# Block two of a two-block metaformer: first scores ahead of the projection, convolution inside the causal attention, combination in nine pieces

## The reference

```python
x = x + _L0_conv_ref(_ln_c(x), ...)      # block one: 7 x 7 neighbourhood attention, 12 heads
t = _to_tokens(x)
t = t + _L0_ffn_ref(_ln_t(t), ...)       # 32 experts, 6 per token, capacity 48, and a shared one
x = _from_tokens(t, x)
x = x + _L1_conv_ref(_ln_c(x), ...)      # block two: full attention within an image, 12 heads
t = _to_tokens(x)
t = t + _L1_ffn_ref(_ln_t(t), ...)       # a causal attention, then 16 experts, 2 per token
```

## Time and profile before

| | |
|---|---|
| median of three runs | 1199.09 us (1198.32 to 1204.48) |
| the profiled execution | 1204.88 us, of which the span 1202.9 us |
| PE busy | 84% of the span |
| DVE, ACT, POOL busy | 60%, 41%, 27% |
| granted clock of PE, mean | 0.945 of full speed |
| chain that ended last | PE 43%, DVE 22%, issue 17%, ACT 6%, POOL 5%, DMA 5% |

### The profile page before, as it was taken

One profiled execution on the slowest core, in us unless ns is written; L12 is line 12 of the kernel. 1 busy time (PEld: TensorE's weight loads), 2 busy tenths in 40 slices (PEclk: granted clock), 3 DMA queues, 4 the chain that ended last, 5 costly groups with the idle time before them and its releaser, 6 DMA issues.

```text
span 1202.9 us, 25715 instructions
## 1 busy us (share of the span) xinstructions
PE 1010.0 (84%) x9398; PEld 789.2 (66%) x9398; DVE 724.5 (60%) x2245; ACT 492.9 (41%) x1223; POOL 319.6 (27%) x514
## 2 busy tenths in 40 slices
PE   4799999999998799788778888787877768989991
PEld 3576776767776545486566657575755547979891
DVE  6586686776774334446576777777776674423334
ACT  1452543643634122115365554555555554212220
POOL 0000000000000470625444554636301120423331
PEclk8999999999998899989899999999997978999996
DMA  9151350540531999600000000000000019698945
GB/s 345 30 150 40 109 148 4 145 140 8 148 110 39 266 364 420 226 1 1 1 2 1 19 1 19 2 19 1 19 1 19 5 34 370 253 396 298 313 148 174
DMA packets 68852, 144.04 MB, mean 120 GB/s; under 512 B 4864, under 2 KB 55184, under 8 KB 66592
## 3 DMA queue, kind: packets, MB, share of 16 engines
q1 hardware_dynamic: 64208, 132.23, 32.5%
q0 software_dynamic: 4560, 10.69, 2.7%
HBM read 96.69 MB, written 46.20 MB: 119 GB/s over the span
## 4 chain that ended last, share of the span: by engine, by line
PE 43%; DVE 22%; issue 17%; ACT 6%; POOL 5%; DMA 5%; POOLq 0%; DVEq 0%; ACTq 0%; SPq 0%
PE bank L1890 8%; DVE neg_max L741 5%; PE bank L641 4%; DMA R<-in_ffn_gu 4%; PE bank L592 4%; PE bank L663 3%; PE bank L705 3%; PE bank L2027 2%; PE bank L1918 2%; POOL sorted_x L1099 2%; PE bank L838 2%; DVE R L714 2%; PE bank L845 2%; ACT R L770 2%; PE bank L671 2%
## 5 line engine op out<-in xcount | busy, mean ns | idle before, releaser
L770 ACT ACTIVATE R<-bank,neg_max 128x128 f32<-128x128 f32 (+2 forms) x576 | 189.1, 404 | 131.4 <-DVE neg_max L741 131.2
L1087 POOL TENSOR_SCALAR R<-cf,ids_rel 128x128 bf16<-128x128 f32 x256 | 168.4, 678 | 39.5 <-PE bank L2007 39.0
L641 PE MATMUL bank<-cf,R 128*128 128x128 f32 x864 | 139.4, 286 | 34.3 <-ACT R L779 20.3
L741 DVE TENSOR_REDUCE neg_max<-bank 128x2 f32<-128x352 f32 (+2 forms) x216 | 129.8, 608 | 29.4 <-PE bank L624 24.0
L641 PEld LDWEIGHTS bank<-cf,R 128*128 128x128 f32 x864 | 98.3, 146 | 56.3 <-ACT R L770 43.2
L1039 POOL TENSOR_TENSOR rstd<-mean_var,cf 128x2 f32<-128x2 f32 x24 | 4.7, 195 | 459.9 <-DVE mean_var L901 459.9
L793 ACT ACTIVATE R<-bank 128x1024 bf16<-128x1024 bf16 x72 | 70.5, 1020 | 74.2 <-PE bank L592 73.9
L1890 PE MATMUL bank<-R 64*116 64x256 f32 (+1 forms) x512 | 97.7, 399 | 0.0
L592 PE MATMUL bank<-cb,R 128*128 128x128 bf16 x1008 | 70.6, 233 | 21.6 <-DVE R L569 21.6
L592 PEld LDWEIGHTS bank<-cb,R 128*128 128x128 bf16 x1008 | 65.1, 105 | 28.9 <-DVE R L569 18.1
L1890 PEld LDWEIGHTS bank<-R 64*116 64x116 f32 (+1 forms) x512 | 65.2, 180 | 26.4 <-issue 16.7
(11 more groups left out here) (258 smaller groups left out, 1908.3 us busy)
## 6 DMA issues: line engine op xcount, KB each, us to landing
R<-in_ffn_w SPq DMA_DIRECT2D x48, 864.0 KB, 7.3
sorted_x<-cmp SPq DMA_DIRECT2D x8, 4128.0 KB, 16.6
R<-in_ffn_gu SPq DMA_DIRECT2D x16, 1392.0 KB, 21.6
R<-in_ffn_dn SPq DMA_DIRECT2D x16, 768.0 KB, 18.4
xs_words<-sorted_x SPq DMA_DIRECT2D x47, 129.0 KB, 5.2
R<-token_y SPq DMA_DIRECT2D x8, 384.0 KB, 6.0
rows<-R SPq DMA_DIRECT2D x8, 224.0 KB, 2.3
out_x<-x_all SPq DMA_DIRECT2D x16, 96.0 KB, 2.5
```

The costliest lines, as they stand in the source:

```text
L641: ins = nc.tensor.transpose(PT[u % 2][:, at + g * P:at + (g + 1) * P], probs[:, u % 3, g * kw + c0:g * kw + c0 + P], ident)
L741: nc.vector.tensor_reduce(neg_max[:, u % 4, 0:g], score_bank(a, u)[:, 0:g * kw].rearrange("p (g k) -> p g k", g=g), AX, ALU.max, negate=Tr ...
L770: ins = nc.scalar.activation(probs[:, u % 3, g * kw:(g + 1) * kw], score_bank(a, u)[:, g * kw:(g + 1) * kw], ACT.Exp, bias=neg_max[:, u % ...
L1087: ins = nc.gpsimd.tensor_scalar(comb_s[i % 2][:, t, j, :], cst("iota_tok"), ids_rel[:, j:j + 1], None, ALU.is_equal)
```

## The change

Block two's order is rewritten on four engines; the arithmetic and the number of its matmuls stay the same.

- The first scores of the next attention (group 0 of CAUSAL, groups 0 and 1 of WINDOW) are issued behind the output's transposes and ahead of `project`; `scores` is lifted out of `attention_pe` for it, with the number already `begun`. CAUSAL's three score banks change places.
- The head transposes are split: one group (8 matmuls) ahead of the last denominators, the rest behind them, one more group behind the projection.
- The combination runs in pieces of 5, 4, 4, 4, 4, 4, 4 and 3 units at groups 2 to 5 instead of three pieces at groups 1 to 3. The wait on `c_slots` moves from the start of `c_window` to the first of these pieces.
- The convolution moves from ahead of the causal attention into its groups 1 to 3, and uses one bank in turn, so its second and third part wait until DVE has read the part before. `w_head` moves with it.
- On DVE `weights` and `sorted_rows` move from the end of `c_causal` into the next `c_window`, behind its group 1; `causal_sums`, `m_rows`, `combine`, `w_norm`, and the reads of the convolution move as well.
- On POOL `c_root` of an image comes ahead of the scatter of the image before it, which it stood behind. On ACT the squares for that root move a group later.

```diff
-            return ((M0, S0, S1) if a is CAUSAL else (S0, S1, M0))[u % 3]
+            return ((S0, M0, S1) if a is CAUSAL else (S0, S1, M0))[u % 3]
...
-        def attention_pe(pe, a, i, extra={}):
+        def scores(pe, a, i, u):
+            t, heads, k0, kw, _, mask = a.groups[u]
+            if u >= 3:
+                await_(pe, a, "exp", i, u - 2)
+
+            if u < 2 or heads[0] % 4 == 0:
+                n = max(heads[0] // 4, u % 2 if u < 2 else 0) + 1
+                await_(pe, a, "qkTa", i, n)
+                await_(pe, a, "qkTd", i, min(n, per_image(a, "qkTd")))
...
             for u in range(a.n + 3):
-                if u < a.n:
-                    scores(u)
+                if begun <= u < a.n:
+                    scores(pe, a, i, u)
...
-            return enumerate((M0, M1) if a is WINDOW and i == 1 else (S0, S1))
+            return enumerate((S0, S1) if a is NEIGH or i == 0 else (M0, M1) if i == 1 else (O1, O1))
...
+                if i >= 2:
+                    c_scatter(i - 2)
...
-                if i >= 1:
-                    c_scatter(i - 1)
+            c_scatter(B - 2)
...
+                    before[1] = lambda: squares("h", i - 1)
+                    before[2] = lambda: c_raw(i)
...
-                    between[0].append(lambda: m_rows(i - 1))
+                    between[0] += qk_copies_dve(dve, WINDOW, i + 1)[2:]
+                    between[0].append(lambda: causal_sums(i - 1))
+                if i >= 2:
+                    between[1].append(lambda: weights(i - 2))
+                    between[1].append(lambda: sorted_rows(i - 2))
+                if i >= 1:
+                    between[2].append(lambda: m_rows(i - 1))
                 if i + 2 < B:
-                    between[3].append(lambda: combine(i + 2))
-                    between[5].append(lambda: w_norm(i + 2))
...
+                    between[6 if i else 3].append(lambda: combine(i + 2))
+                    between[8 if i else 5].append(lambda: w_norm(i + 2))
...
-                at = (1, 2, 4, 5, 6, 7, 8, 8) if i else (5, 6, 6, 6, 7, 7, 8, 8)
+                at = (2, 3, 4, 5, 6, 7, 8, 8) if i else (5, 6, 6, 6, 7, 7, 8, 8)
...
+                    between[0].append(window_sums)
+                    if i + 2 < B:
+                        between[1].append(lambda: conv_qk_dve(dve, WINDOW, brow, i + 2, (0,)))
+                        between[2].append(lambda: conv_qk_dve(dve, WINDOW, brow, i + 2, (1,)))
+                        between[3].append(lambda: conv_v_dve(dve, WINDOW, brow, i + 2))
...
-                if 1 <= i < B - 1:
-                    weights(m)
-                    sorted_rows(m)
...
-                if i >= 2:
-                    pe.wait_ge(s("c_slots"), i - 1)
...
+                def first_unit():
+                    if i >= 2:
+                        pe.wait_ge(s("c_slots"), i - 1)
+                    c_comb(i + 2, 0, 5)
...
-                    for k in range(1, 4):
-                        extra[k] = lambda k=k: piece(k)
-                if i + 2 < B:
-                    extra[(7, "transposed")] = lambda: w_head(i + 2)
+                    extra[1] = lambda: causal_qkv(i)
+                    if i + 2 < B:
+                        extra[2] = first_unit
+                        at = 5
+                        for key, units in (((2, "transposed"), 4), (3, 4), ((3, "transposed"), 4), (4, 4), ((4, "transposed"), 4),
+                                           (5, 4), ((5, "transposed"), 3)):
+                            extra[key] = lambda at=at, units=units: c_comb(i + 2, at, at + units)
+                            at += units
+                        assert at == 2 * NPAIR
                 if i >= 1:
                     extra[(8, "transposed")] = lambda: m_head(i - 1)
-
-                def free(n):
-                    if n == 0 and i + 2 < B:
-                        pe.wait_ge(s("w_xTc"), i + 3)
-                if i >= 0:
-                    extra["weighted"] = lambda: transpose_qk(pe, CAUSAL, i, free, n1=3)
-                attention_pe(pe, WINDOW, i + 1, extra)
+                extra["weighted"] = lambda: transpose_qk(pe, CAUSAL, i, n1=1)
+                extra["turned"] = lambda: transpose_qk(pe, CAUSAL, i, n0=1, n1=3)
+
+                def begin():
+                    scores(pe, CAUSAL, i, 0)
+                    transpose_qk(pe, CAUSAL, i, n0=3)
+                extra["normalised"] = begin
+                attention_pe(pe, WINDOW, i + 1, extra, 2 if i else 0)
                 project(pe, WINDOW, wproj, i + 1)
 
             def c_causal(i):
                 if i < 0:
                     transpose_qk(pe, WINDOW, 1, n0=4)
                     return
-                transpose_qk(pe, CAUSAL, i, n0=3)
+                if i + 1 == B:
+                    transpose_qk(pe, CAUSAL, i, n0=3)
+                extra = {}
+
+                def conv_0():
+                    pe.wait_ge(s("w_xTc"), i + 3)
+                    conv_qk_pe(pe, WINDOW, headT, wqkv, i + 2, (0,))
+
+                def conv_1():
+                    await_(pe, WINDOW, "read", i + 2, 1)
+                    conv_qk_pe(pe, WINDOW, headT, wqkv, i + 2, (1,))
+
+                def conv_2():
+                    await_(pe, WINDOW, "read", i + 2, 2)
+                    conv_v_pe(pe, WINDOW, headT, wqkv, i + 2)
                 if i + 2 < B:
-                    pe.wait_ge(s("w_xTc"), i + 3)
-                    await_(pe, CAUSAL, "qkTa", i, 2)
-                    conv_qk_pe(pe, WINDOW, headT, wqkv, i + 2)
-                    await_(pe, CAUSAL, "qkTa", i, 3)
-                    conv_v_pe(pe, WINDOW, headT, wqkv, i + 2)
-                extra = {}
+                    extra[0] = lambda: w_head(i + 2, O1)
+                    extra[1] = conv_0
+                    extra[2] = conv_1
+                    extra[3] = conv_2
                 if i + 1 == B:
                     extra[0] = lambda: ranks(i - 1)
                 elif i >= 1:
-                    extra[1] = lambda: logits(i - 1)
+                    extra[(1, "transposed")] = lambda: logits(i - 1)
                     extra[(10, "transposed")] = lambda: ranks(i - 1)
                 if i + 1 < B:
                     extra[(9, "transposed")] = lambda: c_head(i + 1)
+                def begin():
+                    scores(pe, WINDOW, i + 2, 0)
+                    transpose_qk(pe, WINDOW, i + 2, n0=4, n1=5)
+                    scores(pe, WINDOW, i + 2, 1)
...
-                    extra["weighted"] = lambda: transpose_qk(pe, WINDOW, i + 2, n1=4)
-                attention_pe(pe, CAUSAL, i, extra)
+                    extra["weighted"] = lambda: transpose_qk(pe, WINDOW, i + 2, n1=1)
+                    extra["turned"] = lambda: transpose_qk(pe, WINDOW, i + 2, n0=1, n1=4)
+                    extra["normalised"] = begin
+                attention_pe(pe, CAUSAL, i, extra, 1 if i + 1 < B else 0)
                 project(pe, CAUSAL, wof, i)
                 if i + 2 < B:
-                    transpose_qk(pe, WINDOW, i + 2, n0=4)
+                    transpose_qk(pe, WINDOW, i + 2, n0=5)
```

More of the change, by code:

```diff
@@ L594, in transpose_qk, with attention_pe @@
                 ins.then_inc(psem("qkT"), 1)
-        def attention_pe(pe, a, i, extra={}):
+        def scores(pe, a, i, u):
[6 more added lines that the diff above has]
+                await_(pe, a, "qkTd", i, min(n, per_image(a, "qkTd")))
+            if a is WINDOW and u == 2:
+                if i == 0:
+                    await_(pe, WINDOW, "read", 1, 2)
+                else:
+                    pe.wait_ge(s("c_u"), nth_square("h", i - 2) if i > 1 else nth_square("u", 0))
+            bank = score_bank(a, u)
+            if mask:
+                nc.tensor.matmul(bank[:, 0:len(heads) * kw], cstb("identb"), cstb(*mask, len(heads) * kw),
+                                 start=True, stop=False)
+            for g, h in enumerate(heads):
+                ins = nc.tensor.matmul(bank[:, g * kw:(g + 1) * kw], q_ap(h, t), k_ap(a, h, k0, kw),
+                                       start=not mask, stop=not mask or g == len(heads) - 1)
+            ins.then_inc(psem("scores"), 1)
+        def attention_pe(pe, a, i, extra={}, begun=0):
             def fill(key):
@@ L1255, in c_causal @@
                 before = {}
+                if i + 2 < B:
+                    before[0] = lambda: w_head(i + 2)
                 if i + 1 < B:
@@ L1628, in c_window @@
                     normed(0)
-                if i >= 1:
+                if i + 1 == B:
                     causal_sums(i - 1)
-                if i + 1 == B:
+                    weights(i - 2)
+                    sorted_rows(i - 2)
                     m_rows(i - 1)
```

60 lines of the change are left out of this document (18 added, 42 removed).

## The result

The changed kernel took 1187.74 us (median of four runs, 1184.68 to 1189.91) beside 1200.7 us for the kernel before: ratio 0.9888, with a 95% interval of 0.9857 to 0.9919. The profiled execution took 1188.06 us with a span of 1186.1. So the change is faster by 1.1%. That is inside the stated range (1186 to 1208), but at rival A's 1187, and outside the 1192 to 1204 that the forecast of 1198 had for itself.

What follows compares the result with a forecast made beforehand. PE was busiest, but DVE's order set the pace at several joints. Five periods at +0.9, -4.4 for image 6 and -1 for image 7 gave -0.9 us: 1198 against the median; own range 1192 to 1204, overall 1186 to 1208.

Steps and rivals of the forecast that it cites:

- rival A: PE's full clock holds through the causal head transposes up to the window's projection; -12.3 us, 1187, chance 0.34.
- steady periods: Images 1 to 5, each 57.83 us in six stretches: +0.9 a period at the lower clock, -1.0 at the full clock.
- Legs 1, 2, 5: Head transposes to causal projection, -0.42; on to first combination matmul, +1.18; window's projection to causal score group 4, -0.2.
- Leg 3: First combination matmul to causal head transposes: 18.79 to 17.4, -1.4, with PE idle about 0.7 and 2.5.
- Leg 4: Causal head transposes to window's projection, 3.67 before: lower clock after thin PE work gives 5.30, +1.63; full clock 3.39.
- Legs 5 and 6: Window's projection to score group 4, -0.2, and on to the next head transposes, DVE-bound, +0.1.
- Rival B: Lower clock also catches head transposes and projection after the causal attention's tail, 1.63 in six periods; 1208, chance 0.24.
- Image 6: No combination here; DVE's 3.08 wait for POOL's root goes, total recovery 5.3; with the period's +0.9, -4.4.
- The slower clock behind the wait: At image 6, an estimated 2.2 us recovered beyond DVE's 3.08 wait for the root.
- Image 7: DVE's 2.96 wait for the root goes, 2.03 of sorting comes in: -1, bounds -2 and +1.
- Image 0: The first image's period, taken at nothing within the -1 for the last image.

Runs made afterwards that it cites:

- sorting back: The changed kernel with weights and sorted_rows returned to the end of c_causal on DVE; 1180.7 us, ratio 0.9832 to the kernel before.
- repeated transposes: The changed kernel with PE repeating m_head's four transposes four more times ahead of the causal head transposes; 1188.67 us, ratio 0.9893 to the kernel before.
- second trace: The changed kernel run once more, unaltered, beside other runs on one chip; 1191.67 us, ratio 0.9906 to the kernel before.
- the convolution later: The changed kernel with the convolution's third part at group 4 instead of 3; 1189.27 us, ratio 0.9907 to the kernel before.
- POOL's order alone: The kernel before with only POOL's order changed, an image's root ahead of the previous image's scatter; 1197.17 us, ratio 0.9958.
- POOL's order of before: The changed kernel with POOL's old order, the root behind the previous image's scatter; 1216.05 us, ratio 1.0115 to the kernel before.

## Why the prediction was right, and where it was not

The direction was right, and so was the range, but the range in part by luck: it reached 1187.74 through rival A, whose condition did not come. The gain came from places that I had put at little, not from the steady periods. In us, for images 1 to 5, 6, 7 and 0, the forecast was 4.5 - 4.4 - 1 + 0 = -0.9. The change's first trace has 1.4 - 5.2 - 3.0 - 3.4 = -10.3 against the kernel before, its second one 3.9 - 6.1 - 2.1 - 3.6 = -8.0.

- **Legs 1, 2, 5** came out within 0.2 us, and leg 2's wait is shown: with the sorting back it goes (6.49 to 5.09). But I counted it in five periods, and at image 1 no rows wait to be sorted: leg 2 is 5.08 there. **Leg 3** was 0.3 longer than forecast, with the two idle gaps as named (0.56 and 1.96 against 0.7 and 2.5).
- **Leg 4** has the forecast's mechanism, shown by the repeated transposes, but its price was too high. I took the 5.30 of image 0, a leg with waits of 0.36 and 0.68 in it, in which the low clock also covered the projection. The new order has no such wait, the low stretch mostly covers the transposes alone, and the leg is 4.54. In the second trace it is 4.54 to 5.52, the last where the low stretch covers the whole leg. In the first trace leg 4 got some 4.4 us longer over five periods, not 8.2 (5 x 1.63). So the five steady periods cost 1.4 us in the first trace and 3.9 in the second, instead of 4.5.
- **Legs 5 and 6** came out as forecast, but "DVE bounds it" is too simple. At image 5, where the clock in the tail stays at 1.00, PE's wait of 0.81 does cost time (the run with the convolution later).
- **Rival A** named nearly the measured time, but the clock did not hold. **Rival B** did not come: leg 1 takes 3.7 to 3.8 in every period of the change's two traces, though the low stretch of the tail moved about.
- **The rule of the Trainium skill** ("TensorE: Matmul & The Clock Gate", section "Why this matters for your kernels"), that single gaps must be short, would have let the clock hold here. From 699.80 the clock is 0.50, behind gaps of 0.56 and 1.96; the measurement decides against the rule in this place.
- **Image 6**: -5.2, and -6.1 in the second trace, against the -4.4 forecast. POOL's swap alone gives 2.3, less than the 3.08 that I took for the least, since a wait of 0.64 is left. The lower clock that I put into its leg 4 did not come (3.33 in both traces). The slower clock behind the wait, which I put at 2.2, did get shorter. The stretches at 0.50, in the kernel before, with POOL's order alone, in the change, and in the change again:

```profile
918.00:931.50 13.50, 9.28 (x69) 5.52 (x70) 10.00 (x28) 7.56 (x24) 0.00 (x0) 0.50 0.01 2
...
916.30:926.50 10.20, 8.48 (x67) 5.12 (x68) 6.46 (x17) 5.75 (x18) 1.15 (x1) 0.50 0.09 28
...
917.70:924.40 6.70, 5.79 (x48) 3.30 (x48) 5.11 (x14) 4.30 (x14) 0.59 (x1) 0.50 0.06 22
...
919.50:922.90 3.40, 3.07 (x27) 1.98 (x28) 2.90 (x6) 2.42 (x9) 0.07 (x1) 0.50 0.11 41
```

The period gets shorter in the same order: 49.51, 47.22, 44.29, 43.39. PE was busy for 9.28 us in the first of these stretches, and for 5.79 and 3.07 in the last two. At the full clock the differences, 3.5 and 6.2, would take at least half as long, so at most 1.7 us of the 5.2 and 3.1 of the 6.1 are the clock's (estimates from these rows). No run took that apart from the other parts of the change.

- **Image 7** is the first mis-sized term: -3.0 instead of -1, and -2.1 in the second trace. I set 2.03 of sorting on DVE against the wait of 2.96. DVE's timeline there:

```profile
953.43 0.16 DVE L1593 TENSOR_TENSOR wsum<-top 128x2 f32<-128x2 f32 x1
...
955.46 0.74 DVE L1519 SCALAR_TENSOR_TENSOR m_rows<-R,rstd,norm_w 128x192 f32<-128x192 f32 x2
```

The sorting runs from 953.43 to `m_rows` at 955.46 while ACT and POOL make the root; it fills the wait instead of adding to it. Here too the clock is low for less: for 20 us in this period of the kernel before (0.50 from 959.0 to 979.3), for 10 and 14 in the change's two traces. What that gave was not taken apart.

- **Image 0** is the other: -3.4 instead of nothing. The run of POOL's order alone has the order of before at image 0, and took 47.53 there instead of 49.75. So 2.2 of it is how long a low stretch lasted (0.50 until about 597 in the kernel before, until about 589 in that run). The other 1.2 is likely the change's order, but the same order took 48.39 in the run with POOL's order of before, with a longer low stretch, and was not tried alone.
- **What the sum missed**: I priced each edit against the kernel before. By the ratios the runs that undo one edit in the change cost 26 us (POOL's order), 13 (scores) and 11 (transposes), far more together than the whole gain. The parts hold each other up, and a price for one of them depends on the others.

Open: what of images 6 and 7 beyond POOL's swap is due to which edit, and how much of it is the clock; what the gain of the early scores is made of; and the 3 us by which the medians and ratios (13.0 and 11.3) show more than the periods of the stage (10.3 and 8.0).

## What to carry to other kernels

When a step is put behind a wait in an in-order queue, ask what must now come earlier to feed that wait. Here early scores, root-first and late denominators hold each other up: undoing one of them cost about as much as the whole change had gained (11 and 13 us), or twice as much (26). Of the three only root-first was tried alone, and it gave 5 us. Put small routing work where its engine stands idle anyway, not behind the work that the next consumer needs: two microseconds of sorting moved back gave 8 us, of which 5.6 are the wait that went in four periods. Before filling a thin place to keep the clock, look where the next low stretch then falls, and how long it gets. And when a change to one engine's wait seems to give nothing, look at the clock of that stretch before calling the wait hidden.

## What was not expected of the hardware

Useless work on TensorE kept its clock at 2.4 GHz (leg 4 from 4.54 to 3.42), and the gain then went to another low stretch 20 us later, 0.9 of 1.12. One program differed by up to 2 us a period from one execution to the next by where its low stretches lay and how long they were (image 4 of the change: 58.14 and 59.96). And the stages behind, the same code in every run, took from 197.5 to 204.4 us, in all runs but one longer where their mean granted clock was lower (0.92 to 0.93 against 0.94 to 0.95).
